# Four graph layers on one core: bf16 node tables in three parts, and 60 tiles read back a step

## The reference

```python
x = _layernorm(x + L0(x, edges, edge_attr_32, ...))   # gather, MLP, sum by dst
x = _layernorm(x + L1(x, src, dst, ...))              # gather by src, sum by dst
x = _layernorm(x + L2(x, edges, W, b))
x = _layernorm(x + L3(x, edges, edge_attr_40, edge_weight, node_type, node_vec, ...))
# L2: row, col = src, dst
msg = norm[:, None] * x[col];  agg = segment_sum(msg, row);  relu(agg @ W.T + b)
# L3: src, dst = edges;  mj = node_mult[dst]
msg = gate * h[dst] * (cw * mj)[:, None]
agg = segment_sum(msg, src) / clip(segment_sum(mj, src), 1e-8)
```

## Time and profile before

| what | value |
|---|---|
| median of 3 runs | 16704.65 us |
| lowest and highest | 16701.4, 16726.7 us |
| profiled execution, span from first to last instruction | 16721.1 us |
| mean granted TensorE clock in it | 0.629 of full speed |
| layer 2, first to last write of GpSimd starts | 8221.8 to 12206.6 us |
| layer 3, the same | 12463.5 to 16455.0 us |
| data moved | 1320.81 MB |

### The profile page before, as it was taken

One profiled execution on the slowest core, in us unless ns is written; L12 is line 12 of the kernel. 1 busy time (PEld: TensorE's weight loads), 2 busy tenths in 40 slices (PEclk: granted clock), 3 DMA queues, 4 the chain that ended last, 5 costly groups with the idle time before them and its releaser, 6 DMA issues. The chain is left out here.

```text
span 16721.1 us, 272828 instructions
## 1 busy us (share of the span) xinstructions
PE 12086.6 (72%) x57442; PEld 11023.7 (66%) x57443; DVE 9036.3 (54%) x22074; ACT 3218.9 (19%) x9623; POOL 12152.9 (73%) x12612
## 2 busy tenths in 40 slices
PE   7888878887666666666533488988863339888886
PEld 6777777777444444444433488888863338888886
DVE  4776766776554444444422366666652126666667
ACT  1111111111211111111111111111113333333331
POOL 4777777777777777777677777777737777777773
PEclk9999999999555555555555555555555555555555
DMA  5444444444333333333211122222221112232221
GB/s 131 101 102 101 102 101 102 101 102 90 91 85 83 87 85 83 87 85 84 64 41 41 52 74 72 74 73 73 73 52 47 47 51 81 74 83 78 78 79 51
DMA packets 1447655, 1320.81 MB, mean 79 GB/s; under 512 B 958662, under 2 KB 1304425, under 8 KB 1443052
## 3 DMA queue, kind: packets, MB, share of 16 engines
q0 software_dynamic: 450320, 493.60, 12.7%
q1 hardware_dynamic: 502094, 520.02, 12.7%
q10 hardware_dynamic: 495148, 306.20, 6.4%
HBM read 903.35 MB, written 415.31 MB: 79 GB/s over the span
## 5 line engine op out<-in xcount | busy, mean ns | idle before, releaser
L1487 POOL DMA_INDIRECT order<-l_msg,l_uring x6250 | 6066.5, 971 | 1918.4 <-issue 1843.4
L1630 PE MATMUL ps<-l_win,l_oht 32*128 x12500 | 2729.8, 413 | 1996.1 <-DMA l_win<-htab 833.9
L1630 PEld LDWEIGHTS ps<-l_win,l_oht 32*128 32x128 f32 x12500 | 2684.0, 327 | 2037.5 <-issue 2037.5
L489 POOL DMA_INDIRECT l_rows<-btab,l_sd x3125 | 2978.1, 953 | 1128.5 <-issue 1099.7
L1027 POOL DMA_INDIRECT l_rows<-y,l_sd x3125 | 2958.1, 947 | 971.7 <-issue 924.7
L1616 PE MATMUL ps<-l_ordb,l_ohs 128*128 128x49 f32 x15040 | 3278.8, 414 | 377.3 <-DVE l_ohs L1516 184.8
L1616 PEld LDWEIGHTS ps<-l_ordb,l_ohs 128*128 128x128 f32 x15040 | 3231.1, 332 | 429.5 <-issue 334.2
L1528 DVE TENSOR_TENSOR acc<-acc,ps 128x49 f32 x7520 | 1524.5, 206 | 1319.2 <-issue 702.1
L630 PE MATMUL ps<-l_rhs,l_lhs 64*128 x6250 | 1422.0, 423 | 652.3 <-DVE l_rows L566 458.5
L630 PEld LDWEIGHTS ps<-l_rhs,l_lhs 64*128 64x128 f32 x6250 | 1350.8, 328 | 713.4 <-issue 713.4
L645 PEld LDWEIGHTS ps<-l_ohe,l_hid 128*128 128x128 f32 x6250 | 1343.0, 332 | 34.8 <-issue 34.1
(11 more groups left out here) (248 smaller groups left out, 10693.5 us busy)
## 6 DMA issues: line engine op xcount, KB each, us to landing
l_ordb<-order SPq DMA_DIRECT2D x752, 250.0 KB
order<-l_msg,l_uring POOLq DMA_INDIRECT x6250
order<-l_zero ACTq DMA_DIRECT2D x125, 775.0 KB, 4.6
l_dstb<-ids SPq DMA_DIRECT2D x376, 200.0 KB
l_eat<-in_ea40P SPq DMA_DIRECT2D x125, 600.0 KB
gates<-l_gate ACTq DMA_DIRECT2D x125, 600.0 KB
l_gin<-gates SPq DMA_DIRECT2D x125, 600.0 KB
l_rows<-btab,l_sd POOLq DMA_INDIRECT x3125
```

What stands on the lines that cost most here:

```text
L489: pool.indirect_dma_start(rows[:, t, :], None, d["btab"], bass.IndirectOffsetOnAxis(ap=sd[:, t, 0:1], axis=0)).then_inc(gat[c], 16)
L1487: pool.indirect_dma_start(d["order"], bass.IndirectOffsetOnAxis(ap=uring[:, t:t + 1], axis=0), msg[:, t, :], None).then_inc(sc[c], 16)
L1630: done = t.matmul(look[c][:, j, :], oht[:, c * CE + j * P:c * CE + (j + 1) * P], win[:, ds((w % 2) * SET + c * LW, LW)], start=False, stop ...
```

## The change

- Tables. y2 and htab are kept as three bf16 parts a row (high, rest, rest of the rest). The parts of a window lie on 96 partitions, one under the other. The ids are broadcast to 96 partitions, the one-hots are 96 x 640 in bf16, and one bf16 matmul a tile sums the three parts. The prologue writes its 32 columns to a table of their own, ptab, which epilogue 1 loads and splits.
- Read-back. RB has six blocks, RT = 60. The parts become (65, 29, 14, 8, 5, 4), the steps 29 + 14 + 8 + 5 + 4 beside groups 65 to 124, and 4 behind: 64 steps. Digits of blocks 0 to 4 stand behind the five takes, those of block 5 behind block 4's. `order` keeps its 3875 tiles (31 cleared a group).
- Zeroing. ScalarE clears agg by four activations between its groups 0 and 1. The five small DMAs go.

```diff
+SPLIT = 3
+WK = SPLIT * WN
-GROUPS = (40, 28, 20, 15, 12, 10)
+GROUPS = (65, 29, 14, 8, 5, 4)
-RB = (10, 10, 10, 10)
+RB = (10, 10, 10, 10, 10, 10)
...
+        ptab=dram("ptab", [NP, G]),
+        y2=dram("y2", [NP, SPLIT, YW], BF16),
+        htab=dram("htab", [NP, SPLIT, MW], BF16),
...
 (pass1)
-                    if part == 0 and c == 0:
+                    if numbering and c == 0:
...
-                    group(g, part, hi <= NB)
+                    group(g, part, hi <= NB, hi <= RT)
...
 (epilogue1: sync, gpsimd, scalar; epilogue2 alike with ht and no pt)
+            sp.dma_start(pt[:, :, :], d["ptab"].rearrange("(b p) f -> p b f", p=P)).then_inc(pt_in, 16)
...
+            g.tensor_tensor(pt[:, :, :], pt[:, :, :], parts[:, :, 0, F:YW], ALU.subtract).then_inc(p_rest, 1)
+            g.tensor_tensor(parts[:, :, 2, F:YW], pt[:, :, :], parts[:, :, 1, F:YW], ALU.subtract).then_inc(p_rest, 1)
...
+            for c in range(n + 2):
+                if c < n:
+                    g.tensor_tensor(y[:, b:b + k, :], x[:, b:b + k, :], per_block(r["dis"][:, b:b + k], k), ALU.mult).then_inc(scaled, 1)
+                if 1 <= c <= n:
+                    take_high(c - 1)
+                if c >= 2:
+                    take_mid(c - 2)
...
+            act.wait_ge(pt_in, 16)
+            nc.scalar.activation(parts[:, :, 0, F:YW], pt[:, :, :], ACT.Copy).then_inc(p_high, 1)
             nc.scalar.activation(root[:, :], deg1[:, :], ACT.Sqrt).then_inc(root_ready, 1)
+            act.wait_ge(p_rest, 1)
+            nc.scalar.activation(parts[:, :, 1, F:YW], pt[:, :, :], ACT.Copy).then_inc(p_mid, 1)
...
 (scatter_pass)
-        win = s.sb("win", [WN, 2 * SET])
-        oht = s.sb("oht", [WN, GE])
+        win = s.sb("win", [WK, 2 * SET], BF16)
+        oht = s.sb("oht", [WK, GE], BF16)
...
-                sp.dma_start(... d["ids16"][0:1, ds(g * GE, GE)].to_broadcast([WN, GE])).then_inc(ids_in, 16)
+                sp.dma_start(... d["ids16"][0:1, ds(g * GE, GE)].to_broadcast([WK, GE])).then_inc(ids_in, 16)
...
-                        sp.dma_start(win[...], table[ds(window_at(nc, pl, starts[c], k), WN), :]).then_inc(win_in, 16)
+                        sp.dma_start(win[...], table[ds(window_at(nc, pl, starts[c], k), WN), :, :].rearrange("n q f -> q n f")).then_inc(win_in, 16)
...
-            for c in range(NCH):
-                pool.dma_start(ordb[0][0:1, c, 0:1], zero[0:1, 0:1]).then_inc(sc[c], 16)
-            pool.memset(agg[:, 0:2 * WIDE], 0.0).then_inc(agg_zero, 1)
...
                     if reading and not head and c <= LAST:
                         block_digits(n, c)
+                        if c == NCH - 1:
+                            for b in range(NCH, len(RB)):
+                                block_digits(n, b)
...
+            with act.Fori(0, 1) as g:
+                group(g, True)
+            for k in range(4):
+                nc.scalar.activation(agg[:, k * (WIDE // 2):(k + 1) * (WIDE // 2)], bc(zero[:, 0:1], [P, WIDE // 2]), ACT.Copy).then_inc(agg_zero, 1)
+            with act.Fori(1, NG) as g:
+                group(g, False)
```

More of the change, by code:

```diff
@@ L851, in pass1 @@
     MOST = max(pl.steps)
-    assert GROUPS[0] == RT
+    assert GROUPS[0] >= RT and pl.begin[2] > GROUPS[0]
     hacc = ps[0:F, 0:NCH * WN].rearrange("p (c n) -> p c n", n=WN)
@@ L1069, in _, with group @@
             dve.wait_ge(none_set, 1)
-            def group(g, part, turning):
+            def group(g, part, turning, numbering):
                 starts, rounds, before, _last = load_group(dve, "dve", pl, r, g)
@@ L1102, in group @@
                     v.tensor_tensor(prod[:, c, :, :], cum, hot[:, c, :, :], ALU.mult).then_inc(cum_read, 1)
-                    if part == 0 and c == 0:
+                    if numbering and c == 0:
                         v.tensor_tensor(begun[:, :, :], first_tile[0:MOST, :, :], bc(tile_no[0:MOST, ds(g, 1)].rearrange("p (q o) -> p q o", o=1), [MOST, PARTS, NB]), ALU.is_le).then_inc(self_blk, 1)
-                    if part == 0 and c == 1:
+                    if numbering and c == 1:
                         dve.wait_ge(self_blk, g + 1)
@@ L1505, in _ @@
             v.tensor_copy(count_row, r["iota_row"][:, :]).then_inc(count_set, 1)
+            for q in range(SPLIT):
+                v.tensor_scalar(in_win[q * WN:(q + 1) * WN, :], r["iota_p"][q * WN:(q + 1) * WN, :], float(-q * WN), None, ALU.add)
             for c in range(NCH):
@@ L1592, in _ @@
                 block_sums(n - 1, LAST)
-                block_digits(n, 1)
-                block_sums(n, 0)
-                block_digits(n, 2)
-                block_sums(n, 1)
-                block_digits(n, 3)
-                block_sums(n, 2)
+                for b in range(1, len(RB)):
+                    block_digits(n, b)
+                    block_sums(n, b - 1)
             block_sums(pl.NS - 1, LAST)
@@ L1649, in _, with group @@
             act.sem_inc(look_zero, NCH)
-            with act.Fori(0, NG) as g:
+            def group(g, head):
                 _starts, _rounds, _before, last = load_group(act, "act", pl, r, g)
@@ L1759, in _ @@
             pool.wait_ge(mult_set, 1)
-            for c, (b, k) in enumerate(runs):
-                pool.wait_ge(normed, c + 1)
-                g.tensor_tensor(ht[:, b:b + k, 0:F], x[:, b:b + k, :], per_block(r["mult"][:, b:b + k], k), ALU.mult).then_inc(y_ready, 1)
+            for c in range(n + 2):
+                if c < n:
+                    b, k = runs[c]
+                    pool.wait_ge(normed, c + 1)
+                    g.tensor_tensor(ht[:, b:b + k, 0:F], x[:, b:b + k, :], per_block(r["mult"][:, b:b + k], k), ALU.mult).then_inc(scaled, 1)
+                if 1 <= c <= n:
+                    b, k = runs[c - 1]
+                    pool.wait_ge(high_made, c)
+                    g.tensor_tensor(ht[:, b:b + k, :], ht[:, b:b + k, :], parts[:, b:b + k, 0, :], ALU.subtract).then_inc(rest_made, 1)
+                if c >= 2:
+                    b, k = runs[c - 2]
+                    pool.wait_ge(mid_made, c - 1)
+                    g.tensor_tensor(parts[:, b:b + k, 2, :], ht[:, b:b + k, :], parts[:, b:b + k, 1, :], ALU.subtract).then_inc(y_ready, 1)
         @block.scalar
@@ L1766, in _ @@
             act.wait_ge(eps_set, 1)
-            for c in range(n + 2):
+            for c in range(n + 5):
                 if c < n:
```

91 lines of the change are left out of this document (64 added, 27 removed).

## The result

The changed kernel takes 17,435.6 us (median of 4, 17,430.6 to 17,441.2) against 16,703.9 for the kernel before: a ratio of 1.0436, 95% interval 1.0423 to 1.0449. The profiled execution has a span of 17,439.4 us.

| stretch, us | before | after | difference |
|---|---|---|---|
| start to epilogue 1 | 8142.9 | 8184.3 | +41.4 |
| epilogue 1 to the first write of layer 2 | 78.9 | 110.7 | +31.8 |
| layer 2, first to last write | 3984.8 | 4357.6 | +372.8 |
| last write of layer 2 to first of layer 3 | 256.9 | 224.7 | -32.2 |
| layer 3, first to last write | 3991.5 | 4349.0 | +357.5 |

A forecast was written before the change was run, and what follows sets the result against it. GpSimd's writes, 31.9 us a group, were taken to bound layers 2 and 3. 470 + 406 - 104 - 4 + 35 = +803 us on the span of 16721.1, less 16.5, gave 17508 us; range 17200 to 17760.

The forecast's parts named there:

- What bounds, and why the saving can't pay: Layers 2 and 3: GpSimd's writes set 31.9 us a group; the look-up's 6.5 us saving is TensorE's, worth nothing.
- The step: Reading groups, walked with TensorE: 39.7 us in layer 2, 38.7 in layer 3, so +470 and +406 us.
- VectorE's own sum: VectorE's step in layer 2: 29.1 us, plus 2.8 for digits and 7.4 for adds, makes 39.3.
- Look-up: TensorE's 25 bf16 matmuls a group: 2.2 us at full clock, at most doubled at half clock, taken as 4.5.
- Tails: Read-back after each layer's last write: 36 blocks become 24 at 4.35 us, -52 us a layer, -104 in both.
- Epilogues: Splitting the tables after layers 1 and 2: lower bound 0, some 40 us at most in layer 1's; sum +35 us.
- Layers 0 and 1: Numbering in layer 1 made for 60 groups instead of 40, beside GpSimd's gathers: 0.
- Rival A: Gaps before VectorE's adds shrink to 0.39 us, the step fits GpSimd's 31.9 us: 16632 us, faster; 7%.
- Rival C: Windows arrive late through SyncE's queue, three times the pieces; were the step 43 us, 17930 us; 4%.
- Rival B: VectorE's register fetch is partly covered, step 34 to 37 us: 16870 to 17220 us; 6%.
- D: No change overall: gains and losses cancel at an excess of 0.6 us a step; 2%.
- The clock: TensorE's read-back: a risen clock would not shorten f32 work, no term; by the skill's rule about 17400 us.

The follow-up runs named there:

- parts40_b: The changed kernel with 40 tiles a step in four blocks (groups 40, 28, 20, 15, 12, 10), run again: 16,817.6 us against 16,731.3, ratio 1.0050.
- early60: The changed kernel with VectorE making the first block's digits before the last adds of the step before: 24,438.8 us, ratio 0.9961, where before took 24,530.7.
- layout: The kernel before with its tables placed in device memory as the change places them, types copied by one transfer: 16,707.0 us against 16,705.3, ratio 1.0001.
- f32_50: The kernel before, f32 look-up kept, with 50 tiles in five blocks and VectorE's order varied by part: 17,029.5 us where before has 16,705.3.
- mixed60: The changed kernel with VectorE's order varied by part (interleaved, early digits, fetch issued twice, as changed): 17,215.6 us where before has 16,701.4.
- weave60: The changed kernel with VectorE's digits interleaved among takes and adds, 60 tiles a step: 24,392.5 us, ratio 0.9946, where before took 24,530.7.
- parts40: The changed kernel with 40 tiles a step in four blocks (groups 40, 28, 20, 15, 12, 10): 24,492.9 us, ratio 0.9984, where before took 24,530.7.

## Why the prediction was right, point by point

- **What bounds, and why the saving can't pay.** Right. parts40_b has the bf16 look-up without the larger steps, keeps GpSimd's step and gains nothing from the look-up.
- **The step.** The walk gave 39.7 and 38.7 us, measured 38.3 and 38.1. The place was right: gaps of 1.55 us and more before the adds, TensorE waiting for adds of block 0. The mis-sized term is where those begin: 20.6 us by the walk, 19.41 in the trace, since the reduce covers their fetch. The groups at the head of a part take about 38.9, not 43.4. With the measured sizes 54 x 6.5 + 4 x 7.1 = 379 us for layer 2, measured +373 (forecast 470); 54 x 6.3 + 4 x 6.6 = 367 for layer 3, measured +358 (406).
- **VectorE's own sum** of 39.3 us is 1.55 too high by the one fetch that the reduce covers; the 37.7 left and VectorE's 0.6 us of waiting for TensorE make the 38.3. It serves while VectorE's fetches stand uncovered, as here and in early60. With them covered it doesn't: interleaved, TensorE's reductions set the 34.3 us.
- **Look-up.** Taken as 4.5 us, it is five times 0.51 us, 2.6, spread over 3.4 by VectorE's comparisons. The doubling was wrong: the row that it started from was already at the pace of 0.50 (its matmuls of 98 columns start 81 ns apart, the look-up's of 80 columns 65). It didn't matter, as said.
- **Tails** forecast -104. The end lost 53.0; in layer 2 the reductions end 112 us after the last write instead of 165, -53. Right.
- **Epilogues** forecast +35. Epilogue 1 measured +31.8 to the first write, where I had 28 less 4 for the memset; epilogue 2 about +20, where I had 7. In epilogue 1 ScalarE waited 28.24 us for ptab, as feared; what the excess in epilogue 2 is made of, I haven't read. (3136 columns are 6.5 times 480, not 6.6; nothing hangs on it.)
- **Layers 0 and 1** forecast 0, measured +41.4: the step "beside GpSimd's gathers: 0" failed. The gathers themselves take 961 and 952 ns in place of 953 and 947, 3125 x 13 ns = 41 us. Neither the tables' places (layout) nor numbering for more groups (f32_50, 952 and 945 ns) does it, each tried by itself. Against these two traces, whose gathers take 952 and 945 ns, the difference is 49 to 51 us. The cause stays open.
- **Sum.** +803 forecast, +718 in the traces: 146 less in the two layers, 41 more in layers 0 and 1, 21 more in the epilogues.
- **Rival A** (covered fetches bring the step to GpSimd's pace): its condition was made in mixed60. The gaps fall to 0.19 us and the step to 34.3, not 31.9, because TensorE's reductions remain.
- **Rival C** (late windows): five window reads take SyncE 5.27 us instead of 2.79, but the look-ups wait for VectorE's l_oht in every row. On the two chips with late loads the kernel before wasn't traced. In weave60, from 13,000 to 17,000 us, windows end nine of the look-up's waits, 301 us in all, and l_oht 275 of them, 855 us: C's place takes part there, but isn't shown to be the bound. **Rival B, D**: not met by the changed kernel; mixed60's interleaved part makes B's condition, and its step of 34.3 us is B's.
- **The clock.** The term of nothing held because TensorE's granted clock, 0.50, never rose in layers 2 and 3. The reason given for it, that a risen clock wouldn't shorten f32 work, is contradicted by the trace. Layer 1 of the kernel before has the same f32 instructions at both levels: six records take 0.77 us in a stretch at 1.00 and 1.35 us at 0.50 (two windows and the tail of layer 2, then TensorE's timeline in the two windows):

```profile
7456.00:7472.00 16.00, 10.74 (x80) 7.29 (x78) 9.85 (x17) 4.74 (x10) 12.16 (x13) 1.00 0.33 104
7480.00:7496.00 16.00, 10.85 (x36) 6.53 (x37) 7.90 (x21) 2.68 (x6) 12.22 (x13) 0.50 0.30 59
12232.00:12371.00 139.00, 137.87 (x640) 136.62 (x639) 109.85 (x352) 0.00 (x0) 0.00 (x0) 0.50 0.20 53
...
7462.62 0.77 PE L1178 MATMUL ps<-l_w,l_sil 97*128 97x96 f32 x6
7487.26 1.35 PE L1178 MATMUL ps<-l_w,l_sil 97*128 97x96 f32 x6
```

## What to carry to other kernels

Work taken from an engine that doesn't set the pace is worth nothing until the batch is sized so that the loop through the engines that get the extra work still fits under the one that does. Walk that loop: when the first consumer can start, what it waits for in the middle, what it needs per block. Then see what the loop waits for next. Here TensorE's first input made first brought its start 4.3 us forward and the step only 1.2, since the first adds still came late. With the other digits moved behind those adds too, as short independent work in front of the register fetches, it was worth 4 us of a 38 us step with no instruction removed.

## What was unexpected of the hardware

- On two chips loads land later: 5.7 to 7.1 us in the median instead of 2.1 from the last window issue to the next load. Instructions take the same time (969 ns a write, 8.76 us for two blocks of reductions), yet the kernel before takes 24,531 us. Layers 0 and 1 suffer as well: in parts40's layer 0 GpSimd waits 2,140 us for the load of the edges' numbers, in the changed kernel's 10 us. There 60 tiles do win (0.9946), by their shorter tails.
- The gathers of layers 0 and 1 take 960 to 962 and 952 to 955 ns in the five traces with the bf16 tables in which loads land in 2.1 us, 952 to 953 and 945 to 947 in the three without, though in layers 0 and 1 nothing in the code differs but the numbering of the read-back's tiles, which f32_50 changed too.
- The load of the weights took SyncE 10.30 us to issue behind the load of the types' table (epilogue 1, as changed).
- f32 matmuls of layer 1 start 110 ns apart at a granted clock of 1.00 and 213 ns apart at 0.50, but after 139 us of f32 reductions without a gap in the tail of layer 2 it still stands at 0.50.
